# Cross-attention keys projected for two batches at once, with the last key of every batch made in the prologue

## Chip, cores and metric

The kernel runs on one core of one Trainium2 chip. The metric is the device time of one launch in microseconds, median of three runs. TensorE does the matrix products, VectorE, ScalarE and GpSimd the elementwise work, SyncE issues the DMAs.

## What is computed

The program adds three blocks to x, of shape 32 × 32 × 512: cross-attention to a context, two retention layers, and a mixture of experts. Only the first is touched by the change:

```python
def proj(x, W, b):
    return (x @ W.T + b).reshape(B, -1, H, D_K).transpose(0, 2, 1, 3)
Q = proj(query, Wq, bq)          # query = layernorm(x): 32 batches of 32 tokens
K = proj(key, Wk, bk)            # key = value = ctx_1024: 32 batches of 257 tokens
V = proj(value, Wv, bv)
scores = jnp.einsum('bhqd,bhkd->bhqk', Q, K) / jnp.sqrt(jnp.float32(D_K))
thr = _softplus_t(raw_thresholds)[None]
scores = jnp.where(scores <= thr, NEG, scores)
attn = jax.nn.softmax(scores, axis=-1)
x = jnp.einsum('bhqk,bhkd->bhqd', attn, V)
return x @ Wo.T + bo             # H = 16 heads of D_K = 32, D_MODEL = 512
```

A context has 257 tokens for each batch, that is 256 and a last one.

## The kernel before

`cross_attention` has a prologue and a loop. In the prologue x is loaded, normalised and transposed, the weights are loaded and split, and the queries of all 1024 tokens are projected (`query(0)` to `query(7)`, eight times 12 matmuls). Every f32 operand of a large product is held as two parts of type fp32r, hi (ScalarE copies it with rounding) and lo (the rest, by a subtraction on VectorE or GpSimd), and `products` (L99) does three matmuls for each of the four 128-row chunks, hi·hi, hi·lo and lo·hi. The value of the last token of all 32 batches is one small group of plain f32 matmuls in the prologue (L765, 32 columns), kept in `vlast`.

The loop goes over eight tiles of 128 tokens, `it`, and in each over four batches, `k` = 0 to 3, with b = 4·it + k. The first and last tile stand outside the hardware loop on some engines. Each engine has its own `body`, and they meet by semaphores alone. For one batch TensorE (`body`, L834) does in this order:

- keys: for each of four 128-row blocks `dc` one group of 12 matmuls of 258 columns (257 tokens and a column of zeros), into banks 0, 1, 4, 5 (L99 with `ctx,wk`);
- the first half of the values, 12 matmuls of 512 columns into bank 0 (L860). Before its last three matmuls stand the waits of `score_waits` and `attend_waits`;
- `score()` for this batch (L826), and `attend()` for batch b − 2 (L811), which writes bank 7;
- the second half of the values into bank 1 (L99 with `wv,ctx`);
- at k = 2 `project()` of the previous tile into bank 7 (L99 with `wo,oT_hl`);
- `turn(b − 1)`: transposes of the normalised probabilities (L791) and of the last token's (L796).

VectorE's body has, in this order: at k = 3 `add_x` (X += bank 7 of the projection, L657, which raises `x1_sum`) and `statistics`; `threshold` of the scores (L622), `softmax_terms`, `heads` of batch b − 2, `last_token` of batch b − 1 (L616, waits for `turn(b − 1)`), `weigh` of batch b (L605, one for each head group, each waits for an exponential) and `reciprocal` (L610). So the weighing of batch b is done while TensorE is in body b + 1, and `add_x` at k = 3 stands behind the weighing of k = 2.

ScalarE copies keys with their bias (L484), values, and transposed probabilities (`turned`, L472), makes the exponentials (L467), and the hi part of the next context (L462) after the key block dc = 1. GpSimd copies the batch's queries (`own_queries`, L358), makes the lo part of the next context (`context_lo`, L353), adds the output bias to X at k = 2, and then normalises the probabilities (L363, which the transposes wait for) and spreads the last token's (L366). SyncE loads one context (514 KB) for each batch into one of two buffers `ctxraw`.

The one wait across tiles that concerns us: at k = 3, `attend()` may write bank 7 only when `add_x` has read the projection from it, so TensorE waits for `x1_sum`:

```python
if c == DC - 1:
    score_waits(b, begin)
    ...
        attend_waits(b - 2, it if k == 3 and not first else None)
```

## Time and profile before

| | us |
|---|---|
| median of three runs | 1652.44 |
| lowest and highest run | 1647.66, 1658.44 |
| the profiled execution, its time | 1651.77 |
| its span in the profile | 1650.0 |
| start of the first keys, end of the loop's last transposes | 42.79, 504.93 |

All numbers on what happens inside are from the one profiled execution, whose time lies 1.8 us above its span. A row of a timeline merges instructions of one kind that follow each other; its second number reaches to the end of the last one, which overlaps the next row, so what a stretch costs TensorE is read from start to start.

### The profile page before, as it was taken

To read this page: it belongs to the slowest core of one execution; us is meant where nothing else is said; L and a number is where in the kernel's file an instruction comes from. 1 tells how busy PE (TensorE), PEld (TensorE's weight loads), DVE (VectorE), ACT (ScalarE), POOL (GpSimd) and SP (SyncE) were. 2 spreads that over 40 slices of the span, in tenths; PEclk is the share of its full clock that TensorE was granted. 3 is DMA by queue.
4 is the path that set the end of the run, shared out by engine and by line. 5 is a ranking of instruction groups with operands and counts; after the bars stand their busy time and mean duration, and the time that the engine had idled before them with its cause. 6 is when DMAs were issued, how large, how long until landed. Compare 5 with 4: busy or idle time off the path is not lost.

```text
span 1650.0 us, 31503 instructions
## 1 busy us (share of the span) xinstructions
PE 1603.8 (97%) x12078; PEld 1347.7 (82%) x12078; DVE 1004.5 (61%) x2002; ACT 848.5 (51%) x1195; POOL 421.0 (26%) x358
## 2 busy tenths in 40 slices
PE   9999999999998999999989999999989999999997
PEld 8888888888886788788877887878877888888886
DVE  5334444443447676544366766444549999989994
ACT  4444454444544333453353333534328788778883
POOL 1333333333333444100014543000021112112111
PEclk9999999999999999999999999999989999999999
DMA  5111111111203100233241002334351554636612
GB/s 202 40 40 30 36 38 38 38 38 30 72 26 111 52 2 1 79 97 93 89 148 52 2 1 77 99 119 129 105 213 20 185 178 156 213 94 236 212 24 71
DMA packets 35839, 143.77 MB, mean 87 GB/s; under 512 B 4976, under 2 KB 5360, under 8 KB 28528
## 3 DMA queue, kind: packets, MB, share of 16 engines
q1 hardware_dynamic: 30592, 130.65, 22.8%
q0 software_dynamic: 5168, 12.06, 3.7%
q8 instruction: 50, 0.82, 0.2%
q14 instruction: 29, 0.24, 0.0%
HBM read 222.39 MB, written 12.85 MB: 143 GB/s over the span
## 4 chain that ended last, share of the span: by engine, by line
PE 59%; DVE 4%; DMA 2%; issue 1%; ACT 1%; SPq 0%; POOL 0%; DVEq 0%; POOLq 0%; ACTq 0%
PE bank L99 36%; PE bank L1654 10%; PE bank L2129 7%; PE bank L1549 2%; PE bank L2135 2%; PE bank L1562 1%; DVE e_w L2056 1%; DMA A<-xh_d,token 1%; PE bank L1638 1%; DMA out<-acc_d 0%; PE bank L1673 0%; DMA wraw<-in_wa 0%; DVE r_wg L1283 0%; DMA acc_d<-A,token 0%; DVE X L1524 0%
## 5 line engine op out<-in xcount | busy, mean ns | idle before, releaser
L2056 DVE TENSOR_TENSOR e_w<-e_raw,e_w 128x2048 fp32r<-128x2048 f32 x134 | 302.2, 2282 | 20.4 <-ACT e_w L1938 19.9
L1938 ACT ACTIVATE e_w<-e_raw 128x2048 fp32r<-128x2048 f32 x134 | 256.7, 1918 | 37.0 <-PE bank L2129 17.7
L99 PE MATMUL bank<-e_w,e_xT 128*128 128x512 f32 x1104 | 272.0, 395 | 0.0
L99 PEld LDWEIGHTS bank<-e_w,e_xT 128*128 128x128 f32 x1104 | 204.4, 189 | 41.5
L99 PE MATMUL bank<-x2T,fw 128*128 128x512 f32 x768 | 187.8, 394 | 5.6 <-DVE fw L1358 5.6
L99 PE MATMUL bank<-ctx,wk 128*128 128x258 f32 x1536 | 191.8, 284 | 0.0
L1654 PE MATMUL bank<-fw,hh 128*128 128x512 f32 x768 | 185.0, 390 | 3.4 <-DVE hh L1476 3.4
L99 PEld LDWEIGHTS bank<-ctx,wk 128*128 128x128 f32 x1536 | 186.4, 192 | 0.2
L99 PEld LDWEIGHTS bank<-x2T,fw 128*128 128x128 f32 x768 | 144.0, 189 | 35.4 <-issue 5.8
L1654 PEld LDWEIGHTS bank<-fw,hh 128*128 128x128 f32 x768 | 143.8, 188 | 34.2 <-issue 2.2
L622 DVE TENSOR_SCALAR_CACHE_REDUCE u<-bank,thr 128x257 f32<-128x257 f32 x128 | 54.5, 482 | 169.4 <-PE bank L826 169.4
L2129 PE MATMUL bank<-e_w,e_hT 128*128 128x512 f32 x552 | 135.7, 395 | 2.3 <-DVE e_hT L2069 2.1
L1198 ACT ACTIVATE hh<-bank 128x512 fp32r<-128x512 f32 x64 | 38.2, 597 | 188.7 <-PE bank L99 188.7
L1476 DVE TENSOR_TENSOR hh<-hf,hh 128x512 fp32r<-128x512 f32 x64 | 46.4, 724 | 145.0 <-ACT hf L1199 145.0
L1907 POOL DMA_INDIRECT acc_d<-A,token x22 | 54.8, 2490 | 312.4 <-ACT A L1959 312.4
L363 POOL TENSOR_TENSOR pr<-pr,rsum 128x1028 f32<-128x1028 f32 x32 | 61.1, 1908 | 283.9 <-DVE rsum L610 283.9
L2129 PEld LDWEIGHTS bank<-e_w,e_hT 128*128 128x128 f32 x552 | 101.8, 188 | 24.2 <-DVE e_hT L2069 3.6
L1133 ACT ACTIVATE xf<-bank,lnv 128x128 f32<-128x128 f32 x124 | 46.7, 463 | 104.5 <-PE bank L1549 104.5
L99 PE MATMUL bank<-wv,ctx 128*128 128x512 f32 x384 | 97.2, 402 | 0.0
L860 PE MATMUL bank<-wv,ctx 128*128 128x512 f32 x384 | 93.3, 391 | 0.0
L1358 DVE TENSOR_TENSOR fw<-fraw,fw 128x1024 fp32r<-128x1024 f32 x64 | 80.3, 1257 | 11.7 <-ACT fw L1150 11.5
L1054 POOL TENSOR_TENSOR r_rstd<-r_veps,mhalf 128x1 f32<-128x1 f32 x32 | 21.0, 656 | 249.9 <-DVE r_veps L1270 189.9
(257 smaller groups left out, 2567.9 us busy)
## 6 DMA issues: line engine op xcount, KB each, us to landing
e_raw<-in_we SPq DMA_DIRECT2D x138, 1024.0 KB, 5.4
fraw<-in_wf SPq DMA_DIRECT2D x64, 512.0 KB, 3.6
ctxraw<-in_ctx SPq DMA_DIRECT2D x32, 514.0 KB, 3.5
wraw<-in_wa SPq DMA_DIRECT2D x20, 512.0 KB, 4.4
X<-in_x SPq DMA_DIRECT2D x4, 512.0 KB, 7.0
acc_d<-X SPq DMA_DIRECT2D x8, 256.0 KB, 3.9
xh_d<-A SPq DMA_DIRECT2D x8, 256.0 KB, 3.0
out<-acc_d SPq DMA_DIRECT2D x4, 512.0 KB, 6.4
```

Source lines behind the costliest of these rows:

```text
L99: last = nc.tensor.matmul(out, lhs(t, a), rhs(t, b), start=start and n == 0, stop=n == len(steps) - 1)
L363: nc.gpsimd.tensor_tensor(pr[:, :, 0:SK], pr[:, :, 0:SK], rsum[:, :].unsqueeze(2).broadcast_to([P, DC, SK]), ALU.mult).then_inc(pn_ok, 1)
L622: nc.vector.tensor_scalar(u[:, g, 0:SK], bank[S_BANK[g]][:, 0:SK], thr[:, g:g + 1], None, ALU.subtract, ALU.max, accum_out=umax[:, g:g + 1 ...
L860: last = nc.tensor.matmul(bank[0][:, :], ctx[k % 2][:, i, c, 0:P], wv[:, j, c, :], start=c == 0 and n == 0, stop=c == DC - 1 and n == len( ...
L1133: nc.scalar.activation(dst[:, c, :], bk[:, c * P:(c + 1) * P], ACT.Identity, scale=lnv[:, name, 0, c:c + 1], bias=lnv[:, name, 1, c:c + 1] ...
L1358: nc.vector.tensor_tensor(fw[k][:, 1, :], fraw[k][:, :], r(fw[k][:, 0, :]), ALU.subtract).then_inc(m["f_lo"], 1)
L1476: nc.vector.tensor_tensor(hh[k % 2][:, 1, :], hf32[k % 2][:, :], r(hh[k % 2][:, 0, :]), ALU.subtract).then_inc(m["h_lo"], 1)
L1654: last = nc.tensor.matmul(bank[4 + j][:, :], hh[k % 2][:, x, j * P:(j + 1) * P], fw[k][:, w, D:2 * D], start=start and i == 0, stop=stop a ...
L1907: nc.gpsimd.indirect_dma_start(out=acc_d[:, :], out_offset=bass.IndirectOffsetOnAxis(ap=token[:, g:g + 1], axis=0), in_=yb, in_offset=None ...
L1938: nc.scalar.activation(w[pos][:, 0, :, :], raw[pos][:, :, :], ACT.Copy).then_inc(m["w_hi"], 1)
L2056: nc.vector.tensor_tensor(w[pos][:, 1, :, :], raw[pos][:, :, :], r(w[pos][:, 0, :, :]), ALU.subtract).then_inc(m["w_lo"], 1)
L2129: last = nc.tensor.matmul(bank[4][:, :], hT[j][:, x, c, :], w[pos][:, y, c, :], start=j == 0 and c == 0 and i == 0, stop=j == 1 and c == D ...
```

## The change

- Contexts are packed in pairs of batches without the last token, 2 × 256 tokens (1024 KB), and loaded, and split into hi and lo, once for a pair.
- At even k the keys are projected for both batches of the pair, 4 × 12 matmuls of 512 columns; at odd k there are no key products and no key copies. The values of each batch are read from its half.
- The keys of the last tokens of all 32 batches are made in the prologue, by 16 plain f32 matmuls of 32 columns between `turn_x(7)` and `query(3)`. VectorE adds the bias (`klast`), and GpSimd puts two of them into `kT` for each pair (`last_keys`).
- `qb` and `kT` hold two batches. GpSimd copies the queries of both at even k. The buffer `u` moves to another place, and the zero columns and their semaphore go.

```diff
-CTX_ROW = 3 * P
+SKM = SK - 1
+NPAIR = NB // 2
...
-                    def load(it, k):
-                        b = BPT * it + k
-                        sp.dma_start(ctxraw[k % 2][:, :, :], ctx_view[bass.ds(b, 1), :, :].rearrange("o p (c n) -> p (o c) n", c=DC)).then_inc(ctx_in[k % 2], 16)
+                    def load(it, half):
+                        sp.dma_start(ctxraw[half][:, :, :], ctx_view[bass.ds(2 * it + half, 1), :, :].rearrange("o p (c n) -> p (o c) n", c=DC)).then_inc(ctx_in[half], 16)
...
-                    for k in range(2, BPT):
-                        sp.wait_ge(ctx_hi, k - 1)
-                        sp.wait_ge(ctx_lo, k - 1)
-                        load(0, k)
                     with sp.Fori(1, NT - 1) as it:
-                        for k in range(BPT):
-                            sp.wait_ge(ctx_hi, BPT * it + k - 1)
-                            sp.wait_ge(ctx_lo, BPT * it + k - 1)
-                            load(it, k)
+                        for half in range(2):
+                            sp.wait_ge(ctx_hi, 2 * it + half - 1)
+                            sp.wait_ge(ctx_lo, 2 * it + half - 1)
+                            load(it, half)
...
-                    def context_lo(it, k, b):
-
-                        pool.wait_ge(ctx_hi, b + 1)
-                        nc.gpsimd.tensor_tensor(ctx[k % 2][:, 1, :, 0:SK], ctxraw[k % 2][:, :, :], r(ctx[k % 2][:, 0, :, 0:SK]),
+                    def context_lo(half, pair):
+
+                        pool.wait_ge(ctx_hi, pair + 1)
+                        nc.gpsimd.tensor_tensor(ctx[half][:, 1, :, :], ctxraw[half][:, :, :], r(ctx[half][:, 0, :, :]),
                                                 ALU.subtract).then_inc(ctx_lo, 1)
 
                     def own_queries(b):
 
-                        nc.gpsimd.tensor_tensor(qb[:, :, :], qT[:, :, bass.ds(b * S, S)], ones[:, :].unsqueeze(1).broadcast_to([P, DC, S]),
-                                                ALU.mult).then_inc(qb_ok, 1)
+                        for i in range(2):
+                            nc.gpsimd.tensor_tensor(qb[:, :, i, :], qT[:, :, bass.ds(b * S + i * S, S)], ones[:, :].unsqueeze(1).broadcast_to([P, DC, S]),
+                                                    ALU.mult).then_inc(qb_ok, 1)
+
+                    def last_keys(b):
+
+                        nc.gpsimd.tensor_tensor(kT[:, :, :, SKM], klast[:, :, bass.ds(b, 2)], ones[:, 0:2].unsqueeze(1).broadcast_to([P, DC, 2]),
+                                                ALU.mult).then_inc(klast_in, 1)
...
                     def body(it, first, last):
                         for k in range(BPT):
                             b = BPT * it + k
-                            if not (first and k == 0):
-                                pool.wait_ge(s_ps, b)
-                            else:
-                                pool.wait_ge(q_ok, 2 * DC)
-                                nc.gpsimd.memset(r(ctx[1][:, :, :, SK:SKE]), 0.0).then_inc(zeroed, 1)
-                            own_queries(b)
-                            if not (last and k == BPT - 1):
+                            if k % 2 == 0:
                                 if not (first and k == 0):
-                                    pool.wait_ge(v_ps, 2 * b)
-                                context_lo(it, k + 1, b + 1)
+                                    pool.wait_ge(s_ps, b)
+                                else:
+                                    pool.wait_ge(q_ok, 2 * DC)
+                                    pool.wait_ge(kl_ok, 1)
+                                own_queries(b)
+                                last_keys(b)
+                                if not (last and k == BPT - 2):
+                                    if not (first and k == 0):
+                                        pool.wait_ge(v_ps, 2 * b)
+                                    context_lo(1 - k // 2, 2 * it + k // 2 + 1)
...
-                    def context_hi(k, use, b):
-                        act.wait_ge(ctx_in[k % 2], 16 * use)
-                        nc.scalar.activation(ctx[k % 2][:, 0, :, 0:SK], ctxraw[k % 2][:, :, :], ACT.Copy).then_inc(ctx_hi, 1)
+                    def context_hi(half, use):
+                        act.wait_ge(ctx_in[half], 16 * use)
+                        nc.scalar.activation(ctx[half][:, 0, :, :], ctxraw[half][:, :, :], ACT.Copy).then_inc(ctx_hi, 1)
...
-                            for dc in range(DC):
-                                act.wait_ge(k_ps, DC * b + dc + 1)
-                                nc.scalar.activation(kT[:, dc, :], bank[K_BANK[dc]][:, 0:SK], ACT.Identity, bias=col("bk", dc)).then_inc(k_ok, 1)
+                            for dc in range(DC if k % 2 == 0 else 0):
+                                act.wait_ge(k_ps, 2 * b + dc + 1)
+                                nc.scalar.activation(kT[:, dc, :, 0:SKM], bank[K_BANK[dc]][:, :].rearrange("p (two n) -> p two n", two=2),
+                                                     ACT.Identity, bias=col("bk", dc)).then_inc(k_ok, 1)
                                 if dc == 0 and k == 2 and not first:
                                     heads_hi(it - 1)
-                                if dc == 1 and not (last and k == BPT - 1):
-                                    context_hi(k + 1, 2 * it + (k + 1) // 2 + 1, b + 1)
+                                if dc == 1 and not (last and k == BPT - 2):
+                                    context_hi(1 - k // 2, it + 1 + k // 2)
...
+                    dve.wait_ge(kl_ps, 1)
+                    nc.vector.tensor_tensor(klast[:, :, :], bank[4][:, DC * NB:2 * DC * NB].rearrange("p (c n) -> p c n", c=DC),
+                                            vec[:, VEC["bk"]:VEC["bk"] + DC].unsqueeze(2).broadcast_to([P, DC, NB]), ALU.add).then_inc(kl_ok, 1)
...
+                    pe.wait_ge(w_in[2], 16)
+                    for dc in range(DC):
+                        for c in range(DC):
+                            last = nc.tensor.matmul(bank[4][:, (DC + dc) * NB:(DC + dc + 1) * NB], raw[2][:, c, dc * P:(dc + 1) * P], craw[:, c, :],
+                                                    start=c == 0, stop=c == DC - 1)
+                    last.then_inc(kl_ps, 1)
...
-                    def score_waits(b, begin):
-
-                        pe.wait_ge(k_ok, DC * b + DC)
+                    def score_waits(it, k, b, begin):
+
+                        if k % 2 == 0:
+                            pe.wait_ge(k_ok, 2 * b + DC)
+                            pe.wait_ge(klast_in, 2 * it + k // 2 + 1)
+                        elif not (isinstance(b, int) and b == 1):
+                            pe.wait_ge(pT_ok, 2 * b - 2)
                         pe.wait_ge(qb_ok, b + 1)
                         if not begin:
                             pe.wait_ge(u_ok, DC * b)
 
-                    def score():
+                    def score(k):
                         for g in range(HPC):
                             rows = slice(g * XD, (g + 1) * XD)
                             for c in range(DC):
-                                last = nc.tensor.matmul(bank[S_BANK[g]][c * S:(c + 1) * S, 0:SK], qb[rows, c, :], kT[rows, c, :], start=True, stop=True)
+                                last = nc.tensor.matmul(bank[S_BANK[g]][c * S:(c + 1) * S, 0:SK], qb[rows, c, k % 2, :], kT[rows, c, k % 2, :], start=True, stop=True)
...
-                            pe.wait_ge(ctx_lo, b + 1)
-                            if first and k < 2:
-                                pe.wait_ge(zeroed, k + 1)
-                            for dc in range(DC):
-                                if dc < 2 and not begin:
-                                    pe.wait_ge(v_ok, 2 * b - 1 + dc)
-                                products(nc, bank[K_BANK[dc]][:, 0:SKE], range(DC), lambda c, h: wk[:, h, c, dc * P:(dc + 1) * P],
-                                         lambda c, h: ctx[k % 2][:, h, c, 0:SKE]).then_inc(k_ps, 1)
-                                if dc == 1 and first and k == 1:
-                                    pe.wait_ge(u_ok, 2)
-                                if dc == 1 and not (first and k < 2):
-                                    pe.wait_ge(pT_ok, 2 * b - 2)
-
-                            pe.wait_ge(k_ok, DC * b + 1)
+                            context = ctx[k // 2]
+                            half = k % 2 * SKM
+                            if k % 2 == 0:
+                                pe.wait_ge(ctx_lo, 2 * it + k // 2 + 1)
+                                for dc in range(DC):
+                                    if dc < 2 and not begin:
+                                        pe.wait_ge(v_ok, 2 * b - 1 + dc)
+                                    products(nc, bank[K_BANK[dc]][:, :], range(DC), lambda c, h: wk[:, h, c, dc * P:(dc + 1) * P],
+                                             lambda c, h: context[:, h, c, :]).then_inc(k_ps, 1)
+                                    if dc == 1 and not begin:
+                                        pe.wait_ge(pT_ok, 2 * b - 2)
+                                pe.wait_ge(k_ok, 2 * b + 1)
+                            else:
+                                pe.wait_ge(v_ok, 2 * b - 1)
                             for c in range(DC):
                                 if c == DC - 1:
-                                    score_waits(b, begin)
+                                    score_waits(it, k, b, begin)
                                     if not (first and k < 2):
                                         if not (first and k == 2):
                                             pe.wait_ge(oT_ok, b - 2)
                                         attend_waits(b - 2, it if k == 3 and not first else None)
                                 for n, (i, j) in enumerate(PARTS):
-                                    last = nc.tensor.matmul(bank[0][:, :], ctx[k % 2][:, i, c, 0:P], wv[:, j, c, :],
+                                    last = nc.tensor.matmul(bank[0][:, :], context[:, i, c, half:half + P], wv[:, j, c, :],
                                                             start=c == 0 and n == 0, stop=c == DC - 1 and n == len(PARTS) - 1)
                             last.then_inc(v_ps, 1)
-                            score()
+                            score(k)
                             if not (first and k < 2):
                                 attend((k - 2) % BPT)
-                            pe.wait_ge(k_ok, DC * b + 2)
-                            products(nc, bank[1][:, :], range(DC), lambda c, h: ctx[k % 2][:, h, c, P:2 * P],
+                            if k % 2 == 0:
+                                pe.wait_ge(k_ok, 2 * b + 2)
+                            else:
+                                pe.wait_ge(v_ok, 2 * b)
+                            products(nc, bank[1][:, :], range(DC), lambda c, h: context[:, h, c, half + P:half + 2 * P],
                                      lambda c, h: wv[:, h, c, :]).then_inc(v_ps, 1)
...
-    cT = ctx.transpose(0, 2, 1).reshape(NB, DC, P, SK).transpose(0, 2, 1, 3)
-    out["ctx"] = cT.reshape(NB, P, DC * SK)
+    cT = ctx[:, :SKM, :].transpose(0, 2, 1).reshape(NPAIR, 2, DC, P, SKM).transpose(0, 3, 2, 1, 4)
+    out["ctx"] = cT.reshape(NPAIR, P, DC * 2 * SKM)
```

TensorE's order around the first values product of k = 3 in the hardware loop, in the kernel before. The names are tiles, `ctx,wk` key products (here from the second of the four blocks on), `wv,ctx` values; brackets hold the semaphores waited for:

```order
L99 MATMUL bank<-ctx,wk 128x258 [waits v_ok]
L99 MATMUL bank<-ctx,wk 128x258 x11
L849 REGISTER_ALU
L99 MATMUL bank<-ctx,wk 128x258 [waits pT_ok]
L99 MATMUL bank<-ctx,wk 128x258 x23
L851 ISA
L860 MATMUL bank<-wv,ctx 128x512 [waits k_ok]
L860 MATMUL bank<-wv,ctx 128x512 x8
L817 REGISTER_ALU
L801 REGISTER_ALU [waits u_ok,oT_ok,qb_ok,k_ok]
L860 MATMUL bank<-wv,ctx 128x512 [waits x1_sum,v_ok,pT_ok]
L860 MATMUL bank<-wv,ctx 128x512 x2
```

The same place after the change, from the last transpose of k = 2 (`ident,plast`) to the scores (`kT,qb`) and the attention products (`pT,v`):

```order
L812 MATMUL bank<-ident,plast 128x128 [waits olast_ok,plast_ok]
L871 ISA
L880 MATMUL bank<-wv,ctx 128x512 [waits v_ok]
L880 MATMUL bank<-wv,ctx 128x512 x8
L837 REGISTER_ALU
L838 REGISTER_ALU [waits pT_ok]
L840 REGISTER_ALU [waits qb_ok]
L817 REGISTER_ALU [waits oT_ok,u_ok]
L880 MATMUL bank<-wv,ctx 128x512 [waits x1_sum,v_ok,pT_ok]
L880 MATMUL bank<-wv,ctx 128x512 x2
L846 MATMUL bank<-kT,qb 32x257 x16
L827 MATMUL bank<-pT,v 32x32 x32
```

The key products between the transposes of k = 2 and the values of k = 3 are gone, and the wait for `x1_sum` stands where it stood, ahead of the last three matmuls of the first values product.

VectorE at the same place, rows of the kernel before, from the last of the weighing of k = 2 to the thresholds of k = 3:

```order
L605 SCALAR_TENSOR_TENSOR pr,psums<-u,floor,ex 128x257 [waits ex_ok] x2
L609 REGISTER_ALU
L610 RECIPROCAL rsum<-psums 128x4 [waits pr_ok]
L657 ISA [waits o_ps,x1_ok]
L657 TENSOR_TENSOR X<-bank,X 128x512
L662 ISA [waits x1_sum]
L662 BN_STATS x_stats<-X 128x6
L620 REGISTER_ALU
L622 TENSOR_SCALAR u,umax<-bank,thr 128x257 [waits s_ps]
```

The addition to X that raises `x1_sum` (L657) stands behind the weighing and the reciprocal of batch k = 2. After the change VectorE has the same instructions here, nine lines further down in the file.

## Rows read from the trace of the kernel before

**Rows 1.** The page, busy time of the engines.

```profile
PE 1603.8 (97%) x12078; PEld 1347.7 (82%) x12078; DVE 1004.5 (61%) x2002; ACT 848.5 (51%) x1195; POOL 421.0 (26%) x358
```

**Rows 2.** Waits of TensorE, 40 to 520 us, the longest: total, times, longest.

```profile
PE bank L791 <- POOL pr L363: 1.4, 1, 1.4
```

**Rows 3.** Timeline of TensorE, one batch (k = 2): start, us, instructions.

```profile
240.69 6.00 PE L99 MATMUL bank<-ctx,wk 128*128 128x258 f32 x48
246.52 2.91 PE L860 MATMUL bank<-wv,ctx 128*128 128x512 f32 x12
249.36 0.72 PE L826 MATMUL bank<-kT,qb 32*32 32x257 f32 x32
...
250.71 3.04 PE L99 MATMUL bank<-wv,ctx 128*128 128x512 f32 x12
253.59 2.88 PE L99 MATMUL bank<-wo,oT_hl 128*128 128x512 f32 x12
256.31 1.03 PE L791 MATMUL bank<-ident,pr 128*128 128x128 f32 x8
...
257.33 4.92 PE L99 MATMUL bank<-ctx,wk 128*128 128x258 f32 x39
```

**Rows 4.** Timeline of TensorE, prologue.

```profile
12.21 5.54 PE L765 MATMUL bank<-craw,raw 128*128 128x32 f32 x32 [0.24 <-DMA raw<-in_xwv]
17.56 4.48 PE L99 MATMUL bank<-xT,wq 128*128 128x512 f32 x12
...
29.07 13.88 PE L99 MATMUL bank<-xT,wq 128*128 128x512 f32 x60
42.79 5.92 PE L99 MATMUL bank<-ctx,wk 128*128 128x258 f32 x48
```

**Rows 5.** Busy time in windows: the column PEclk is the granted clock.

```profile
core 0: us, PE busy (x) PEld busy (x) DVE busy (x) ACT busy (x) POOL busy (x), PEclk, DMA share, GB/s
13.00:13.60 0.60, 0.60 (x8) 0.60 (x7) 0.60 (x3) 0.57 (x2) 0.00 (x0) 1.00 1.15 437
...
14.20:15.00 0.80, 0.80 (x6) 0.80 (x5) 0.80 (x5) 0.04 (x1) 0.00 (x0) 0.50 1.11 458
...
20.50:21.00 0.50, 0.50 (x3) 0.36 (x3) 0.09 (x1) 0.00 (x0) 0.00 (x0) 0.79 1.16 362
...
509.00:510.00 1.00, 0.22 (x2) 0.22 (x3) 1.00 (x1) 0.45 (x1) 0.92 (x2) 1.00 0.00 0
```

**Rows 6.** Timeline of TensorE, router products near the end of the retention layers.

```profile
1193.28 0.96 PE L1673 MATMUL bank<-rw,xf 128*128 128x8 f32 x8
1194.09 0.91 PE L92 MATMUL bank<-ident 128*128 128x128 f32 x6
```

**Rows 7.** Timeline of VectorE behind the transposes that end at 257.33.

```profile
257.70 0.29 DVE L616 TENSOR_TENSOR olast<-bank,vlast 128x128 f32<-128x128 f32 x1 [4.64 <-PE bank L796]
258.55 0.49 DVE L605 SCALAR_TENSOR_TENSOR pr<-u,floor,ex 128x257 f32<-128x257 f32 x1 [0.56 <-ACT ex L467]
...
260.76 0.69 DVE L657 TENSOR_TENSOR X<-bank,X 128x512 f32 x1
```

**Rows 8.** Timelines of ScalarE and GpSimd, prologue and the same stretch.

```profile
35.41 1.91 ACT L409 ACTIVATE wk<-raw 128x2048 fp32r<-128x2048 f32 x1
...
42.99 0.69 ACT L425 ACTIVATE qT<-bank,vec 128x512 f32<-128x512 f32 x1 [2.03 <-PE bank L99]
...
257.92 2.07 ACT L467 ACTIVATE ex<-u,nb,sc 128x257 f32<-128x257 f32 x4
...
260.86 1.06 ACT L462 ACTIVATE ctx<-ctxraw 128x1028 fp32r<-128x1028 f32 x1
...
263.36 0.47 ACT L484 ACTIVATE kT<-bank,vec 128x257 f32<-128x257 f32 x1 [0.96 <-PE bank L99]
...
260.81 1.90 POOL L363 TENSOR_TENSOR pr<-pr,rsum 128x1028 f32<-128x1028 f32 x1 [10.06 <-DVE rsum L610]
...
263.58 2.21 POOL L353 TENSOR_TENSOR ctx<-ctxraw,ctx 128x1028 fp32r<-128x1028 f32 x1
```

More of the change, by code:

```diff
@@ L209, in cross_attention @@
         qT = sb("qT", [P, DC, TOK])
-        sb("after_qT", [P, DC, TOK])
+        ctxraw = [sb(f"ctxraw{i}", [P, DC, 2 * SKM]) for i in range(2)]
         raw = [None] + [sb(f"raw{i}", [P, DC, D]) for i in (1, 2)]
-        ctx = [sb("ctx0", [P, 2, DC, CTX_ROW], F32R)]
-        ctxraw = [sb(f"ctxraw{i}", [P, DC, SK]) for i in range(2)]
+        ctx = [sb("ctx0", [P, 2, DC, 2 * SKM], F32R)]
+        u = sb("u", [P, DC, SKE])
         pT = sb("pT", [P, 2, DC, P])
@@ L216, in cross_attention @@
         wo = sb("wo", [P, 2, DC, D], F32R)
-        qb = sb("qb", [P, DC, S])
-        sb("after_qb", [P, DC, 2 * P - S])
+        qb = sb("qb", [P, DC, 2, S])
+        sb("after_qb", [P, DC, 2 * P - S - S - NB])
+        klast = sb("klast", [P, DC, NB])
         raw[0] = sb("raw0", [P, DC, D])
@@ L243, in cross_attention @@
             oT = sbi("oT", [P, DC, P])
-            kT = sbi("kT", [P, DC, SK])
+            kT = sbi("kT", [P, DC, 2, SK])
             plast = sbi("plast", [P, HPC, XD])
@@ L254, in cross_attention @@
             ctx_in = [sem("ctx_in0"), sem("ctx_in1")]
-            ctx_hi, ctx_lo, zeroed = sem("ctx_hi"), sem("ctx_lo"), sem("zeroed")
+            ctx_hi, ctx_lo = sem("ctx_hi"), sem("ctx_lo")
             x_in = [sem(f"x_in{i}") for i in range(4)]
@@ L263, in cross_attention @@
             vl_ps, vl_ok = sem("vl_ps"), sem("vl_ok")
+            kl_ps, kl_ok, klast_in = sem("kl_ps"), sem("kl_ok"), sem("klast_in")
             th_act, th_dve = sem("th_act"), sem("th_dve")
@@ L310, in _ @@
                     load(0, 1)
-                    for k in range(2, BPT):
-                        sp.wait_ge(ctx_hi, k - 1)
-                        sp.wait_ge(ctx_lo, k - 1)
-                        load(0, k)
                     with sp.Fori(1, NT - 1) as it:
-                        for k in range(BPT):
-                            sp.wait_ge(ctx_hi, BPT * it + k - 1)
-                            sp.wait_ge(ctx_lo, BPT * it + k - 1)
-                            load(it, k)
+                        for half in range(2):
+                            sp.wait_ge(ctx_hi, 2 * it + half - 1)
+                            sp.wait_ge(ctx_lo, 2 * it + half - 1)
+                            load(it, half)
                     sp.wait_ge(w_hi, DC + 3)
                     sp.wait_ge(w_lo, DC + 3)
-                    for k in range(BPT):
-                        sp.wait_ge(ctx_hi, BPT * (NT - 1) + k - 1)
-                        sp.wait_ge(ctx_lo, BPT * (NT - 1) + k - 1)
-                        load(NT - 1, k)
-                        ahead_load(k)
+                    for half in range(2):
+                        sp.wait_ge(ctx_hi, 2 * (NT - 1) + half - 1)
+                        sp.wait_ge(ctx_lo, 2 * (NT - 1) + half - 1)
+                        load(NT - 1, half)
+                        ahead_load(2 * half)
+                        ahead_load(2 * half + 1)
                     sp.wait_ge(v_ps, 2 * NB)
@@ L780, in _ @@
                     pe.wait_ge(vl_ok, 1)
+                    pe.wait_ge(kl_ok, 1)
                     pe.wait_ge(w_lo, DC + 2)
```

8 lines of the change are left out of this document (3 added, 5 removed).

## Prediction

> **What bounds the kernel now.** I read the busy table first: TensorE is busy for 1603.8 of 1650.0 us [rows 1], so the question is what it does with its time. Second, its waits over the whole cross-attention, 40 to 520 us: the longest is 1.4 us, once, for the last batch's probabilities behind the loop [rows 2]. Inside the loop TensorE waits for nobody, and one body follows the other without a gap. Third, the timeline of TensorE for one batch [rows 3]. From start to start the keys take 246.52 − 240.69 = 5.83 us (48 matmuls of 258 columns), the first half of the values 2.84, the scores and the attention products together 1.35, the second half of the values 2.88, the output projection (only at k = 2) 2.72, and the transposes of the probabilities end at 257.33, where the next keys start. So time is won only by less TensorE work, and lost by any wait that the shorter bodies uncover. The softmax chain of VectorE, ScalarE and GpSimd runs beside it and costs nothing as long as its results come before TensorE asks. That is what has to be looked at, because after the change the bodies of odd k have no key products in front of them.
>
> **Keys for two batches at once (saves).** A pair of batches had 2 × 48 matmuls of 258 columns and has 48 of 512. Before: 2 × 5.83 = 11.66 us. The nearest row for a long run of 512-column products on alternating banks is the query projection: 60 of them from 29.07 to 42.79, 13.72 us, 228.7 ns each [rows 4]. 48 of them are 10.98 us. The columns alone fall by under 1% (516 to 512); the gain is mostly that 258 columns at 5.83 / 48 = 121.5 ns cost more than half of 228.7 ns. Saved: 0.68 us a pair. The values of odd k now follow transposes and no longer keys; the product in that position took 2.88 us instead of 2.84 [rows 3], so I give back 0.04. 16 × 0.64 = 10.2 us. Ends: by the output projection's pace (2.72 for 12, 10.88 for 48) 16 × 0.78 = 12.5; by the pace of the second half of the values (2.88, 11.52 for 48) 16 × 0.14 = 2.2. I take 10.2, since the query run is the one of the same form.
>
> Here the Trainium skill says otherwise (TensorE: Matmul & The Clock Gate, section "Wait — 56ns, not 53.3ns?"): back to back, a warm matmul costs its columns at 2.4 GHz and a fixed 2.5 ns or so. By that rule the change would save (4 × 1/2.4 + 2.5) × 768 = some 3.2 us (an estimate from the page). The rows give a larger fixed part, since 2 × 121.5 − 228.7 = 14.3 ns go with each merged pair of matmuls; the sum goes by the rows.
>
> **Last keys in the prologue (costs).** 16 matmuls of 32 columns in plain f32 go in before the fourth query product, 32 records as for the last values' group of the same form [rows 4]. TensorE is not idle anywhere from there to the loop (60 query products in one run, then keys), so this is paid in full; what ScalarE and VectorE do for the weights in that stretch follows the query products and moves with them. Price: plain f32 matmuls with a full weight load each are in the router rows, 8 in 1194.09 − 1193.28 = 0.81 us, 101 ns each [rows 6]; 32 make 3.2 us. The same form itself took 17.56 − 12.21 = 5.35 us, but mostly at half clock [rows 4, 5]; that is the upper end, and 0.81 × 4 = 3.2 is also the lower. I take 3.2.
>
> **Splitting and copying in pairs (hidden).** ScalarE: one split of 2048 elements takes 1.91 us (the weight split) for two of 1.06, and a copy of 512 columns with its bias 0.69 for two of 257 at 0.47 [rows 8]: less work in all, beside TensorE's 11 us of keys. GpSimd: the split of 1028 took 2.21 us [rows 8], so 2048 take some 4.4, once in a pair; the two query copies and the last-key copy handle 128 and 8 elements in a partition and are small beside it. The split follows the previous normalisation and the ScalarE split, so by my estimate it runs from about 8 to 12.4 us after the start of an even body of 19 us, and the next normalisation is wanted only in the odd body. Its output is wanted 13 us later. The context loads are half as many and twice as large, with some 30 us each. I put all of this at nothing; if the GpSimd order did push the normalisation, it would show as a wait of the transposes.
>
> **What is late in the odd bodies.** I go through TensorE's waits there, with t = 0 at the end of the transposes. The probabilities of the last batch are weighed by VectorE from 258.55 − 257.33 = 1.2, and GpSimd's normalisation ends at 260.81 + 1.90, t = 5.4 [rows 7, 8]. The transposes that want it come after values, scores, attention products and values: 2.88 + 1.35 + 2.88 = 7.1. That is close, but in time by 1.7 us. The copies of the transposed probabilities are over before ScalarE's exponentials start at 257.92, t = 0.6 [rows 8]; they are wanted at t = 2.2. One wait does not fit. At k = 3 TensorE waits, ahead of the last quarter of the first values product, until VectorE has added the previous tile's projection to X (`x1_sum`), because the attention products are to overwrite bank 7. VectorE does that first in its body of k = 3, which means behind weigh and reciprocal of batch k = 2: it ran from 260.76 to 261.45, which is t = 4.12 [rows 3, 7]. Before the change TensorE came to the wait at 5.83 + 9/12 × 2.84 = 8.0, long after. Now it comes at 9/12 × 2.88 = 2.16. So it stands for 4.12 − 2.16 = 1.96 us, in each of the seven iterations that have a previous tile: 13.7 us. Behind the wait hang three value products, the scores, and the softmax of that batch, none of which is wanted earlier. Ends: nothing, if something lets VectorE come before TensorE, and 13.7; I take 13.7, since the chain that holds the add back (copies, exponentials, weigh) is the same as before. At k = 1 there is no such wait.
>
> **Sum.** −10.2 + 3.2 + 13.7 = +6.7 us on the profiled execution's 1651.77 us: 1658.5. The median of the runs shown is 1652.44, 0.7 us above that execution, so 1659 for a median; the shown runs spread from 1647.66 to 1658.44.
>
> **Rivals.**
> - *The wait is not there or is short.* If the add came by t = 2.2, the sum would be −10.2 + 3.2 = −7.0, 1645. For it: TensorE's loop shows no wait at all before. Against it: VectorE's order is unchanged, and the weigh in front of the add is bound to exponentials that can't start before the copies. 11%.
> - *The clock falls behind the wait (slower).* In the prologue the granted clock went from 1.00 to 0.50 between 13.6 and 14.2 while TensorE showed no gap, in the 32-column matmuls that follow a few short idle stretches, and came back at about 20.7 [rows 5]: some 7 us at 1.2 instead of 2.4 GHz, 3.5 us lost. The odd body of k = 3 has 2 us of idle time, three products, scores and attention products on 32-row pieces, so it could do the same. Each fall costs 3.5 us; all seven make 1658.5 + 24.5 = 1683, and from three of them on the kernel is over 1% slower. Against it: at 509 to 510 TensorE was busy for 0.22 us with more idle around, and the clock stayed at 1.00 [rows 5]. 10%. The Trainium skill (same page, Part 1: The HAM clock gate) ties the clock to how busy TensorE was lately; the fall at 13.6 shows here that records without a gap are not enough for that.
> - *The fixed part of a matmul is small.* If 512 columns behave so that a pair saves only the 0.14 of the lower end, the sum is −2.2 + 3.2 + 13.7 = +14.7, 1667: still within 1%. 6%. By the Trainium skill's figure above (same page and section) the time would be 1651.8 − 3.2 + 3.2 + 13.7, some 1665 (an estimate).
> - *Nothing I have a row for* would bring over 1% (16.5 us): even the best ends, −12.5 + 3.2, do not. 2%.
>
> My forecast has 71%. Its own bounds are −12.5 + 3.2 + 13.7 = +4.4 and −2.2 + 5.4 + 13.7 = +16.9. The range 1648 to 1669 takes in these, a part of the case without the wait, and one to three clock falls. About 1% is what a measurement of this kernel can tell from no change, 1636 to 1669. Faster by over 1%: 3%. Within 1%: 86%. Slower: 11%.
>
> **What would show it.** Right: in the changed profile the keys of a pair take 10.9 to 11.1 us from start to start; TensorE's waits have VectorE's add to X at seven times some 1.9 us, and hardly anything else; the prologue's keys start at about 46 us instead of 42.79; the cross-attention ends some 6.7 us later. Wrong: no wait for that add; a wait of the transposes for GpSimd's normalisation; keys of a pair above 11.5 us; a granted clock under 1.00 between 46 and 505 us; or a wait of the first keys for the GpSimd split.

## The result, and the profile after

The changed kernel takes 1668.07 us, median of four runs (1666.18 to 1671.15), against 1652.82 before: a ratio of 1.0095, interval 1.007 to 1.012. It is 15.2 us slower, where 6.7 were forecast on the profile. Its profiled execution took 1666.18 us with a span of 1664.4, so 14.4 us above the span before.

TensorE's waits over the same stretch as in [rows 2], kernel after (total, times, longest):

```profile
PE bank L880 <- DVE X L666: 13.6, 7, 2.0
PE bank L807 <- POOL pr L366: 0.5, 1, 0.5
```

Nearly the whole list is a wait that was not there before: seven times for VectorE's addition to X, 13.6 us. (The wait of 1.4 us in [rows 2] is still there, but at 524 us now and so behind this stretch.) The values' records have a new gap. Timeline of TensorE, kernel after, from the output projection at k = 2 to the next keys, which answers to [rows 3] (start, us, instructions, in brackets the idle time and what ended it):

```profile
203.02 2.89 PE L100 MATMUL bank<-wo,oT_hl 128*128 128x512 f32 x12
205.75 1.03 PE L807 MATMUL bank<-ident,pr 128*128 128x128 f32 x8
206.62 0.39 PE L812 MATMUL bank<-ident,plast 128*128 128x128 f32 x2
206.76 2.31 PE L880 MATMUL bank<-wv,ctx 128*128 128x512 f32 x9
211.04 0.93 PE L880 MATMUL bank<-wv,ctx 128*128 128x512 f32 x3 [1.96 <-DVE X L666]
211.91 0.72 PE L846 MATMUL bank<-kT,qb 32*32 32x257 f32 x32
212.55 1.10 PE L827 MATMUL bank<-pT,v 128*32 128x32 f32 x64
213.58 4.09 PE L100 MATMUL bank<-wv,ctx 128*128 128x512 f32 x12
217.51 1.03 PE L807 MATMUL bank<-ident,pr 128*128 128x128 f32 x8
```

Nine of the twelve value products run, then TensorE stands for 1.96 us. The first values product takes 211.91 − 206.76 = 5.15 us from start to start. At k = 1 the same product also follows transposes, and waits for nothing:

```profile
90.29 2.99 PE L880 MATMUL bank<-wv,ctx 128*128 128x512 f32 x12
93.21 0.72 PE L846 MATMUL bank<-kT,qb 32*32 32x257 f32 x32
```

It takes 2.92 us there. So 2.23 us are lost at the wait, of which 1.96 is recorded as idle and 0.27 goes as TensorE runs empty and starts again. The seven waits cost 15.3 us in this way, 13.6 of them idle. And behind this wait something else is off: the attention products took 1.03 instead of 0.70 us, and the second half of the values 3.93 instead of 2.88. The windows of the same stretch show why (busy time of each engine, then the granted clock, the DMA share and GB/s):

```profile
core 0: us, PE busy (x) PEld busy (x) DVE busy (x) ACT busy (x) POOL busy (x), PEclk, DMA share, GB/s
205.00:211.00 6.00, 4.08 (x23) 3.15 (x22) 3.12 (x11) 3.04 (x6) 0.75 (x1) 1.00 0.00 0
211.00:213.00 2.00, 1.96 (x68) 1.17 (x72) 0.88 (x2) 0.00 (x0) 1.56 (x2) 0.88 0.00 0
213.00:216.00 3.00, 3.00 (x55) 2.45 (x46) 2.46 (x14) 0.60 (x1) 0.00 (x0) 0.51 0.00 0
216.00:218.00 2.00, 2.00 (x13) 1.66 (x12) 0.00 (x0) 0.29 (x1) 0.00 (x0) 1.00 0.00 0
```

The clock stayed at 1.00 through the wait itself and fell to half 1.5 us after its end, while TensorE was busy again with scores and attention products, and was back by 216. This happened behind four of the seven waits (those that end at 211, 331, 392 and 512 us). At the other three of these four the clock fell 0.9 to 1.6 us after the end of the wait. Over the four, the second halves of the values lost 3.5 us, the attention products 1.3 and the scores 0.8: 5.6 us.

The chain on VectorE that holds the wait, kernel after, beside [rows 7]:

```profile
207.14 0.29 DVE L625 TENSOR_TENSOR olast<-bank,vlast 128x128 f32<-128x128 f32 x1 [4.64 <-PE bank L812]
208.00 0.49 DVE L614 SCALAR_TENSOR_TENSOR pr<-u,floor,ex 128x257 f32<-128x257 f32 x1 [0.57 <-ACT ex L472]
...
210.20 0.69 DVE L666 TENSOR_TENSOR X<-bank,X 128x512 f32 x1
```

It is the chain of before, shifted: the addition ends 4.1 us behind the transposes. The prologue, kernel after, beside [rows 4]:

```profile
28.80 3.66 PE L788 MATMUL bank<-craw,raw 128*128 128x32 f32 x32
32.29 13.86 PE L100 MATMUL bank<-xT,wq 128*128 128x512 f32 x60
45.99 11.04 PE L100 MATMUL bank<-ctx,wk 128*128 128x512 f32 x48
56.87 2.88 PE L880 MATMUL bank<-wv,ctx 128*128 128x512 f32 x12
```

The loop starts 3.2 us later. The group of the last keys took 3.49 us; the products ahead of it ended 0.3 us earlier than before. The first keys of a pair take 56.87 − 45.99 = 10.88 us, the later ones 10.99.

From the first keys to the start of the loop's last transposes (`ident,plast`) it is 461.9 us before and 473.2 after, 11.3 more. It is made of −10.8 (keys: 186.6 us in all before, 175.7 after), +0.6 (the first halves of the values, 2.92 us behind transposes and 2.81 behind keys, where all took 2.84), +15.3 (the waits with their restarts), +5.6 (the four falls of the clock), and +0.6 for one wait in the first tile, where the transposes of the first batch stood 0.48 us for GpSimd's normalisation.

### The profile page after: what moved, and what is told of

Its sections match the earlier page's. It is cut to its first block, busy times and chain, and to the rows that moved or that the text cites. A ratio compares the mean times of both kernels' runs of the same rounds, so it can differ in the third digit from the quotient of the medians.

```text
span 1664.4 us, 29796 instructions
## 1 busy us (share of the span) xinstructions
PE 1602.6 (96%) x11342; PEld 1312.2 (79%) x11342; DVE 1002.2 (60%) x2003; ACT 836.4 (50%) x1115; POOL 427.7 (26%) x356
## 4 chain that ended last, share of the span: by engine, by line
PE 59%; DVE 4%; DMA 2%; issue 1%; ACT 1%; SPq 0%; POOL 0%; DVEq 0%; POOLq 0%; ACTq 0%
PE bank L100 36%; PE bank L1677 10%; PE bank L2152 7%; PE bank L1572 2%; PE bank L2158 2%; PE bank L1585 1%; DVE e_w L2079 1%; DMA A<-xh_d,token 1%; PE bank L1661 1%; DMA out<-acc_d 0%; PE bank L1696 0%; DVE r_wg L1306 0%; DMA wraw<-in_wa 0%; DMA acc_d<-A,token 0%; DVE X L1547 0%
## 5 line engine op out<-in xcount | busy, mean ns | idle before, releaser
L100 PE MATMUL bank<-ctx,wk 128*128 128x512 f32 x768 | 178.3, 391 | 0.0
L100 PEld LDWEIGHTS bank<-ctx,wk 128*128 128x128 f32 x768 | 143.1, 188 | 29.1
L880 PE MATMUL bank<-wv,ctx 128*128 128x512 f32 x384 | 95.6, 395 | 13.6 <-DVE X L666 13.6
L100 PE MATMUL bank<-wv,ctx 128*128 128x512 f32 x384 | 100.6, 412 | 0.0
L880 PEld LDWEIGHTS bank<-wv,ctx 128*128 128x128 f32 x384 | 70.5, 188 | 30.0 <-issue 16.3
L1381 DVE TENSOR_TENSOR fw<-fraw,fw 128x1024 fp32r<-128x1024 f32 x64 | 80.3, 1257 | 11.7 <-ACT fw L1173 11.4
```

The lines of the kernel that those rows point to most:

```text
L100: last = nc.tensor.matmul(out, lhs(t, a), rhs(t, b), start=start and n == 0, stop=n == len(steps) - 1)
L880: last = nc.tensor.matmul(bank[0][:, :], context[:, i, c, half:half + P], wv[:, j, c, :], start=c == 0 and n == 0, stop=c == DC - 1 and n ...
L1381: nc.vector.tensor_tensor(fw[k][:, 1, :], fraw[k][:, :], r(fw[k][:, 0, :]), ALU.subtract).then_inc(m["f_lo"], 1)
```

## Experiments

Theory A was: the new wait for `x1_sum` costs its idle time, a restart and the falls of the clock behind it; the keys save what they should. Its rivals were that the short odd bodies bring on the falls by themselves (B), and that the loss is in the 512-column products (C). All times are compared with the kernel before on the same chip, 29 runs of it with the first four experiments (median 1652.83) and 21 with the last three, on another chip (1652.08). The changed kernel was not run again beside them; where a time is set against its 1668.07, that is the value above. A loop's length is taken as above, and each is from one profiled execution.

### The addition early

```diff
                             if k == BPT - 1 and not first:
-                                add_x(it - 1)
                                 statistics(it - 1)
...
                                 last_token(b - 1)
+                            if k == 2 and not first:
+                                add_x(it - 1)
```

> The changed kernel with one move: the addition of the projection to X (which raises x1_sum) stands at k = 2, between last_token and weigh, and no longer at k = 3 behind weigh and reciprocal. The same work is done. Theory A (the wait for this addition costs its idle time, a restart of TensorE, and brings on the falls of the clock behind it): the seven waits go, the clock stays at 1.00 through the loop, and the time falls by 16 us for the waits and 5 us for the falls, to about 1647, some 6 us below the kernel before. Theory B (the clock falls because the short odd bodies have less dense work): the waits go but three to five falls stay, 1652. Theory C (the loss is in the 512-column key products themselves): nothing much changes, 1665 or more.

Measured: 1650.66 us (12 runs), ratio 0.9993, interval 0.9977 to 1.0009. The list of waits, over the same stretch:

```profile
PE bank L808 <- POOL pr L366: 2.5, 2, 2.0
PE bank L828 <- ACT pT L477: 0.4, 1, 0.4
PE bank L813 <- POOL plast L369: 0.3, 1, 0.3
```

The seven waits are gone (the 2.0 us in the first line lie behind the loop), and the same place reads, in TensorE's timeline:

```profile
204.31 0.39 PE L813 MATMUL bank<-ident,plast 128*128 128x128 f32 x2
204.46 2.99 PE L881 MATMUL bank<-wv,ctx 128*128 128x512 f32 x12
207.38 0.72 PE L847 MATMUL bank<-kT,qb 32*32 32x257 f32 x32
208.03 0.78 PE L828 MATMUL bank<-pT,v 128*32 128x32 f32 x64
208.74 3.06 PE L100 MATMUL bank<-wv,ctx 128*128 128x512 f32 x12
```

Twelve value products in one piece, 2.92 us, and the attention products at 0.70 again. The window of the whole loop has the clock at 1.00, where the changed kernel's has 0.99:

```profile
46.00:498.00 452.00, 451.52 (x4868) 360.65 (x4867) 187.63 (x789) 205.32 (x336) 170.75 (x134) 1.00 0.10 35
```

The loop is 452.7 us long: 9.2 below the kernel before and 20.5 below the changed one. The wait and the low clock are gone together. C falls, and by the profile B falls too: neither this loop nor those of the three later kernels that stand on the early addition has a stretch of low clock. The time alone would not decide between A and B, since 1650.7 lies nearer to B's 1652 than to A's 1647. The median is 17.4 us below the changed kernel, but only 2.2 below the kernel before, where A had expected 6, and the interval allows no difference at all.

A part of what is missing stands in this profile. Its span is 1646.1 us, 3.9 below the kernel before, where loop and prologue give 9.2 − 3.0 = 6.2. The other 2.3 us are lost behind the loop. There TensorE waits for GpSimd's normalisation of the last batch, and the clock falls behind the wait:

```profile
504.29 1.09 PE L808 MATMUL bank<-ident,pr 128*128 128x128 f32 x8 [2.04 <-POOL pr L366]
505.00:510.00 5.00, 4.75 (x86) 4.12 (x85) 2.81 (x5) 3.73 (x8) 0.58 (x1) 0.66 0.52 197
```

Before, this wait was 1.41 us and the clock behind it stayed at 1.00. From the loop's last transposes to the output projection behind the loop it is 14.6 us here (498.50 to 513.12) and was 13.2 (504.70 to 517.89), so 1.4 of the 2.3 us go here. All four profiles with the early addition show the same wait of 2.04 us, the fall behind it and 14.6 to 14.7 us; in the other five the wait is 1.40 to 1.69 us, the clock stays at 1.00, and it takes 13.2 us (13.5 with the addition in the middle). Why the wait is longer was not tested. It fits that VectorE comes to the last batch's thresholds 2.4 us after the start of the scores (495.78), and came 0.9 us after it before. The remaining 0.9 us are lost later, where the falls of the clock lie elsewhere in each profile.

The profiled execution was one of the fast ones, too: 1647.91 us against a median of 1650.66. The mean granted clock over the twelve runs is 0.9860, against 0.9886 over the 29 of before; 0.0026 of 1650 us are 4.3 us of full-speed time, and a fall like the one behind the loop is 1.7 of them. Where the clock falls in the executions that were not profiled, no run here shows.

### The same move in the kernel before

The edit is the same, in the kernel before.

> The kernel before with the same move of the addition to X. There TensorE comes to the wait at 8 us, when the addition has been done in either place. Theory A: no wait, no change, within 0.3% of the kernel before. If the place of the addition were worth something by itself (rival), this one would be faster by several us too.

Measured: 1653.25 us (10 runs), ratio 0.9997, interval 0.9981 to 1.0014, and a loop of 461.9 us, to the first decimal that of the kernel before. The move is worth nothing where TensorE comes to the wait late; it is worth 17 us in the changed kernel.

### The wait filled with work

```diff
                                 if c == DC - 1:
+                                    if k == 3 and not first:
+                                        pe.wait_ge(v_ok, 2 * b)
+                                        for _ in range(8):
+                                            nc.tensor.matmul(bank[1][:, 0:P], ident[:, :], ident[:, :], start=True, stop=True)
                                     score_waits(it, k, b, begin)
```

> The changed kernel with eight products of the identity with itself (16 records, some 1.9 us at full clock) put ahead of the wait for x1_sum at k = 3, into bank 1, which is free there. The wait itself stays as long as it is. Theory A (idle time brings on the falls of the clock): the clock stays at 1.00 in all seven places, the falls' 5 us come back, about 1662. Theory B (the falls have to do with scores and attention products, not with idle time): the falls stay, 1667 to 1669.

Measured: 1663.74 us (6 runs), ratio 1.0066, interval 1.0039 to 1.0093. Timeline of TensorE at the same place:

```profile
208.67 2.31 PE L884 MATMUL bank<-wv,ctx 128*128 128x512 f32 x9
210.82 1.95 PE L877 MATMUL bank<-ident 128*128 128x128 f32 x16
212.94 0.93 PE L884 MATMUL bank<-wv,ctx 128*128 128x512 f32 x3 [0.17 <-DVE X L666]
213.80 0.72 PE L846 MATMUL bank<-kT,qb 32*32 32x257 f32 x32
```

The values' last three products still start 4.3 us behind the first, as before the filling (4.28), so the wait costs as much. But the clock is at 1.00 in the whole loop:

```profile
48.00:515.00 467.00, 465.46 (x4979) 373.57 (x4978) 189.85 (x793) 205.26 (x336) 170.74 (x134) 1.00 0.10 34
```

The attention products take 0.70 us in all batches, and the loop is 467.8 us. That is 5.4 below the changed kernel, where the rows gave 5.6 for the falls, and 15.1 above the early addition, which is what the seven waits cost without any fall. The time is near A's 1662, though its interval reaches up to 1668, into B's range; the profile decides. So the falls need the idle time: scores and attention products alone do not bring them on. Whether idle time followed by dense work would do it, no run here shows.

### The keys in halves

```diff
-                                    products(nc, bank[K_BANK[dc]][:, :], range(DC), lambda c, h: wk[:, h, c, dc * P:(dc + 1) * P],
-                                             lambda c, h: context[:, h, c, :]).then_inc(k_ps, 1)
+                                    products(nc, bank[K_BANK[dc]][:, 0:SKM], range(DC), lambda c, h: wk[:, h, c, dc * P:(dc + 1) * P],
+                                             lambda c, h: context[:, h, c, 0:SKM])
+                                    products(nc, bank[K_BANK[dc]][:, SKM:2 * SKM], range(DC), lambda c, h: wk[:, h, c, dc * P:(dc + 1) * P],
+                                             lambda c, h: context[:, h, c, SKM:2 * SKM]).then_inc(k_ps, 1)
```

This stands on the early addition.

> The early addition, and the keys of a pair as 96 products of 256 columns in place of 48 of 512; columns are the same. If the saving is a fixed cost of each matmul (my step: 14 ns a pair of matmuls), the keys of a pair take 11.5 to 11.7 us from start to start and the kernel loses 8 to 11 us against the one with the early addition alone, about 1657. If the saving were only the columns that went (516 to 512), the keys stay at 11.0 us and the time at about 1647.

Measured: 1662.05 us (8 runs), ratio 1.0047, interval 1.0027 to 1.0068. Timeline of TensorE, one pair's keys:

```profile
187.71 11.75 PE L100 MATMUL bank<-ctx,wk 128*128 128x256 f32 x96
199.29 2.91 PE L883 MATMUL bank<-wv,ctx 128*128 128x512 f32 x12
```

96 products of 256 columns take 11.58 us, 120.6 ns each; 48 of 512 took 10.99, 229.0 each. The columns are the same, so 2 × 120.6 − 229.0 = 12 ns go with each merged pair. Over the sixteen pairs these are 9.6 of the 10.8 us that the keys saved, so the saving is mostly one of instructions; the rest goes with the columns, 516 for 512. The loop is 462.8 us, 10.1 longer than with whole keys, and with that no shorter than before the change. The Trainium skill (TensorE: Matmul & The Clock Gate, section "Wait — 56ns, not 53.3ns?") gives a warm matmul a fixed part of about 2.5 ns on top of its columns. The 12 ns measured here differ from it; the measurement decides.

This profile shows one thing more. In the prologue the clock fell at the end of the last keys' group, which ran from 28.8 to 32.5:

```profile
28.80:32.00 3.20, 3.20 (x32) 3.20 (x30) 0.69 (x1) 2.74 (x3) 0.38 (x1) 1.00 0.00 0
32.00:33.00 1.00, 1.00 (x6) 1.00 (x6) 0.25 (x1) 0.00 (x0) 1.00 (x1) 0.53 0.00 0
33.00:35.00 2.00, 2.00 (x6) 1.52 (x5) 0.04 (x1) 0.00 (x0) 2.00 (x1) 0.50 0.00 0
35.00:36.00 1.00, 1.00 (x5) 0.82 (x4) 0.00 (x0) 0.00 (x0) 1.00 (x1) 0.76 0.00 0
```

TensorE shows no gap in it; the group is 32 products of 32 columns each behind a full weight load. Part of the profiled execution's 1666.11 us is this, and it can be part of the median too, which is 11.4 us above the early addition, where 8 to 11 were expected; so the 10.1 us are taken from the loop.

### The addition in the middle

```diff
-                    def weigh(b):
+                    def weigh(b, groups):
...
-                        for c in range(DC):
+                        for c in groups:
...
-                                add_x(it - 1)
...
-                            weigh(b)
+                            weigh(b, range(2))
+                            if k == 2 and not first:
+                                add_x(it - 1)
+                            weigh(b, range(2, DC))
                             reciprocal(b)
```

> The changed kernel with the addition to X between the second and the third weighing instruction at k = 2, so about 1.0 us earlier than in the changed kernel and later than in the early one. Theory A (the wait's length decides): seven waits of 0.7 to 1.1 us in place of 1.96, and fewer falls of the clock behind them than the four of seven seen (none to two); the time lies between the two, 1654 to 1659. Rival (any gap at this place costs a restart and a fall, whatever its length): 1663 or more, with falls in four places.

Measured: 1656.2 us (10 runs), ratio 1.0023, interval 1.0007 to 1.0039. The wait and the place:

```profile
PE bank L882 <- DVE X L666: 4.5, 7, 0.6
```

```profile
210.40 2.31 PE L882 MATMUL bank<-wv,ctx 128*128 128x512 f32 x9
213.36 0.93 PE L882 MATMUL bank<-wv,ctx 128*128 128x512 f32 x3 [0.65 <-DVE X L666]
214.23 0.71 PE L848 MATMUL bank<-kT,qb 32*32 32x257 f32 x32
```

Seven waits of 0.65 us, no fall of the clock in the loop, and a loop of 458.6 us, 5.8 above the early one: 0.83 us a wait. The values product takes 214.23 − 210.40 = 3.83 us, 0.91 above the 2.92 without a wait, so the restart is 0.26 us, as behind the long wait. The time lies between, as the length of the wait says, though the idle time came out just under the 0.7 to 1.1 that I had expected. (The last keys' group brought a fall in this profile too, a longer one, from about 33.4 to 40 us; the group ended at 34.5.)

### Without the last keys, and with the last keys spread

The first leaves out the sixteen products and makes `klast` from x, so its output is another; the second keeps them, and moves VectorE's addition of their bias behind the lo parts of two more weights:

```diff
-                    dve.wait_ge(kl_ps, 1)
...
+                    dve.wait_ge(kl_ps, DC)
...
-                    for dc in range(DC):
+                    def last_key(dc):
...
-                    last.then_inc(kl_ps, 1)
+                        last.then_inc(kl_ps, 1)
...
+                    last_key(0)
                     query(3)
                     pe.wait_ge(xT_lo, NT)
                     for n in range(4, 8):
+                        if n < 7:
+                            last_key(n - 3)
                         query(n)
```

> The early addition, and without the sixteen f32 products of the last keys in the prologue; klast is made from x instead, so the last token's keys are not computed and the output is another. Theory A (the group costs its 3.5 us and, in some runs, a fall of the clock behind it, as in the profile of the kernel with halved keys, from 32 to 36 us): faster than the early one (1650.7) by 3.3 us and up to 3.6 more, 1644 to 1647; the mean granted clock, 0.9866 over the early one's runs, goes back to 0.988 to 0.989. Theory B (the group costs its own time alone): 1647.4, the clock stays at 0.9866.

> The early addition, and the group of the last keys cut into four of 0.9 us, one ahead of each of the query products 3 to 6, with VectorE's bias addition behind its second weight. The same work. Theory A (a long stretch of sparse products brings on the falls in the prologue): no fall there in any profile, the time falls below the early one's 1650.7 by 1 to 4 us, and this is the best version with the reference's output. Theory B (no falls from this group): within 1 us of 1650.7.

Measured: without them 1645.38 us (5 runs), ratio 0.996, interval 0.9947 to 0.9974; spread 1648.63 us (11 runs), ratio 0.9984, interval 0.9973 to 0.9995. In the profiles the loop starts at 42.33, 46.25 and, with the early addition alone, 45.76 us, so the group costs 3.4 us and spreading it does not make it cheaper.

From 1650.66 to 1645.38 are 5.3 us, 1.9 more than that, and inside A's range. But the two were measured on different chips, and against the kernel before on the same chip it is 6.7 and 2.2, so 4.5 us. And the mean granted clock without the group is 0.9866, hardly above the 0.9860 with it (which the expectation had as 0.9866) and below the 0.9887 of before, so the second half of A is not borne out. The group does bring on a fall in some executions (two of the five profiled ones that have it in one piece), but most of the clock lost against the kernel before is lost elsewhere. One such place is the fall behind the loop, which both of these profiles have: its 1.7 us are 0.0010 of the mean clock.

With the group spread, the one profile has no fall in the prologue from 26 to 46 us, and the mean clock is 0.9871. The gain over the early addition is 2.0 us between medians, 1.3 when each is set against its own chip's kernel before, and the two intervals overlap. So whether spreading helps stays open. What is shown is that this version, early addition and spread last keys, is faster than the kernel before by 0.16% (0.05 to 0.27%). It is the best version found that does all the work.

## Why the prediction was right, and where it was short

- *What bounds the kernel.* Right. TensorE had no wait in the loop, and the time follows its work and its one new wait.
- *Keys of a pair.* 0.67 us saved a pair against 0.68 by the timelines, 10.8 us in all. The values of odd k took 2.92 us instead of 2.84, against 0.04 given back, and those of even k 2.81. Together that is 10.2 us saved, as in the sum; that the two errors in the values cancel is chance. The source (a fixed cost of each matmul) is shown by the keys in halves.
- *Last keys in the prologue.* The group took 3.49 us against 3.2. The price came from router products of 8 columns at 101 ns; with 32 columns they take 109. The loop still starts 3.2 us later, as forecast, because the products ahead of the group ended 0.3 us earlier in this execution. The sum left out that such a group can bring on a fall of the clock, although it noted that the values' group had one.
- *Splitting and copying in pairs.* Hidden, as said: no wait for the split in the whole loop, whose lo part takes 4.6 us on GpSimd. One wait of the transposes, 0.48 us in the first tile, was not seen, and it costs 0.6. The first batch has no attention products and no transposes ahead of its own, so it is shorter from its scores to its transposes: 9.9 us without the wait (59.68 to 69.5), against 12.4 for the third batch (85.05 to 97.44).
- *The wait for `x1_sum`.* Its place, its cause, its count and its idle time (13.7 forecast, 13.6 measured) were right, and the experiment with the addition early shows the cause. The step that was mis-sized is "it stands for 1.96 us": a wait in the middle of a run costs its idle time and a restart of some 0.25 us. The seven cost 15.3 us, 1.6 above the term.
- *The clock.* This rival took part in the result, beside the forecast and not in its place. It was priced at 3.5 us a fall and stood at nothing in the sum. The clock fell in four places of seven, at 1.4 us each: the price was carried over from the prologue, where the low clock lasted some 7 us, and here it was back after 3.4. These 5.6 us are the largest part of what my sum is short; the filled wait shows that they hang on the idle time. What I held against the rival, that the clock stayed at 1.00 at 509 to 510 in spite of a wait, did not carry over to this place.
- *The sum.* 6.7 forecast against 14.4 on the profiles and 15.2 on the medians, so the sum held less than half of the loss. The 7.7 on the profiles are falls 5.6, restarts 1.6 and the first tile's wait 0.6, less 0.1 elsewhere. Two of the signs that I had named for being wrong did come: a granted clock under 1.00 in the loop, and a wait of the transposes for GpSimd's normalisation. The time lay inside the range, near its upper end of 1669. That end stood there for slower keys and a dearer prologue (+16.9), which did not come, and for up to three falls at 3.5 us, where four came at 1.4. That it held is in part luck.

## What to carry to other kernels

When work is taken out from in front of a wait, look up, on the other engine, when its release really comes, not whether the wait shows today: this one had 4 us of slack that only the key products gave. If it turns up, try to move the releasing instruction forward on its own engine before anything else; here one line moved ahead of the weighing cost nothing in the loop and gave back 17 us. Then look at the next wait on the way, for with the loop's wait gone another one behind the loop grew from 1.4 to 2.0 us, and the clock fell behind it. And count a wait in a dense run of TensorE as more than its idle time: a restart, and the clock of the sparse work behind it.

## What was not expected of the hardware

- Merging two matmuls of 256 columns into one of 512 saved 12 ns of 241, with a weight load for each; the operands were fp32r throughout.
- A wait in the middle of the values product cost some 0.25 us beyond its idle time, behind 1.96 us of idle time (0.27) as behind 0.65 (0.26).
- An idle stretch of 1.96 us followed by scores and attention products on 32-row pieces brought the granted clock from 1.00 to 0.5 in four places of seven; 0.65 us of idle time at the same place, or the same stretch filled with products of 128 columns, did so in none. Behind the loop, a wait of 2.04 us for the last batch brought a fall in four profiles of four, and the same wait at 1.40 to 1.69 us in none of five.
- The clock also fell in a stretch where TensorE showed no gap at all, within the last microsecond or so of 32 plain f32 products of 32 columns (3.5 us long), in two of five profiles.
- Runs of one kernel differ along with their mean granted clock: with the addition early, the five runs at 0.984 took 1653.4 to 1655.1 us, and the six at 0.987 to 0.989 took 1646.6 to 1650.4.
